# A banded retention layer with an FP4 feed-forward: corner blocks and the last 64 feed-forward columns packed into two passes, and value tiles split in eight steps

## The reference

```python
# x = X;  GAMMA = 0.9;  ln = layer norm without weights
Q, K, V = xpos(ln(x) @ W_Q), xpos(ln(x) @ W_K, downscale=True), ln(x) @ W_V
p = softmax(Q @ K.T) * 0.9 ** abs(n - m)        # decay AFTER the softmax
x = x + p @ V
g, u = fp4(ln(x)) @ fp4(w_gate).T, fp4(ln(x)) @ fp4(w_up).T   # 256 -> 704
x = x + fp4(silu(g) * u) @ fp4(w_down).T                       # 704 -> 256
# fp4: blocks of 16 columns share a scale max|x|/6, values rounded to 0,.5,1,1.5,2,3,4,6
```

## Time and profile before

| | |
|---|---|
| median of 3 runs | 2677.11 us (2676.68 to 2681.3) |
| the profiled execution | 2681.48 us, of which the span is 2679.4 us |
| PE matmul / weight load busy | 97% / 87% of the span |
| DVE / ACT / POOL busy | 81% / 57% / 67% |
| granted TensorE clock | 0.994 of full speed over the span |
| DMA | 184.11 MB, queue busy 19.9% of 16 engines |
| chain that ended last | PE 69%, POOL 8%, issue 4%, DVE 3%, ACT 2% |

### The profile page before, as it was taken

The page is one execution under the profiler, slowest core; times in us unless marked ns, Lnnn a source line. Parts: engine busy times, 40 slices in busy tenths (PEclk is TensorE's granted clock), DMA queues, the critical chain, the costliest instruction groups (busy, mean ns, idle before and its releaser), DMA issues.

```text
span 2679.4 us, 51414 instructions
## 1 busy us (share of the span) xinstructions
PE 2610.4 (97%) x16418; PEld 2343.5 (87%) x16418; DVE 2173.3 (81%) x4784; ACT 1514.3 (57%) x2936; POOL 1794.8 (67%) x1635
## 2 busy tenths in 40 slices
PE   8999999999999999999999999999999999999997
PEld 7888789988998889988998899888998899889986
DVE  8999777778888888788888888788878888888885
ACT  5666555555555555555555555555555555565553
POOL 6999846667666666666666666666666666666664
PEclk9999999999999999999999999999999999999998
DMA  7878400121001300120002100130013001210000
GB/s 275 288 274 284 177 13 23 30 91 41 25 27 32 103 25 19 33 101 29 25 31 91 40 25 27 32 103 25 19 33 102 28 25 33 91 39 25 27 24 17
DMA packets 136033, 184.11 MB, mean 69 GB/s; under 512 B 10080, under 2 KB 93152, under 8 KB 135776
## 3 DMA queue, kind: packets, MB, share of 16 engines
q1 hardware_dynamic: 135776, 180.85, 19.9%
HBM read 103.22 MB, written 77.59 MB: 67 GB/s over the span
## 4 chain that ended last, share of the span: by engine, by line
PE 69%; POOL 8%; issue 4%; DVE 3%; ACT 2%; POOLq 0%; DVEq 0%; ACTq 0%
PE score L420 21%; PE acc L539 17%; PE ring L420 15%; PE acc L420 8%; PE ring L512 5%; PE ring L557 3%; POOL vals L838 2%; POOL h_buf L877 2%; POOL probs L856 2%; POOL hq_buf L881 1%; PE ring L504 1%; POOL xv L862 1%; DVE smax L1079 1%; ACT probs L703 1%; ACT hT L673 1%
## 5 line engine op out<-in xcount | busy, mean ns | idle before, releaser
L856 POOL TENSOR_TENSOR probs<-probs,decay 128x512 f32<-128x512 f32 (+3 forms) x432 | 523.9, 1229 | 437.7 <-ACT probs L703 437.7
L420 PE MATMUL score<-keys,q_st 128*128 128x512 f32 x3072 | 770.8, 400 | 6.0 <-ACT probs L703 3.2
L420 PEld LDWEIGHTS score<-keys,q_st 128*128 128x128 f32 x3072 | 561.2, 189 | 122.5 <-issue 3.6
L539 PE MATMUL acc<-vals,pT 128*128 128x256 f32 x4416 | 588.9, 285 | 1.6 <-DVE pT L1066 1.6
L539 PEld LDWEIGHTS acc<-vals,pT 128*128 128x128 f32 x4416 | 552.7, 189 | 14.3 <-DVE pT L1066 2.9
L420 PE MATMUL ring<-w_gu,xqT 128*128 128x512 f32 (+1 forms) x2304 | 508.6, 374 | 0.0
L1079 DVE TENSOR_REDUCE smax<-score 128x1 f32<-128x1024 f32 x256 | 313.2, 1224 | 220.1 <-PE score L420 218.3
L673 ACT ACTIVATE pT<-ring 128x512 fp32r<-128x512 f32 (+3 forms) x432 | 226.7, 535 | 451.1 <-PE ring L512 443.6
L420 PEld LDWEIGHTS ring<-w_gu,xqT 128*128 128x128 f32 x2304 | 419.2, 188 | 62.1
L862 POOL TENSOR_TENSOR xv<-xv,xe 128x256 f32<-128x256 f32 x128 | 94.4, 737 | 336.1 <-DVE xv L935 336.1
L1066 DVE TENSOR_TENSOR pT<-ring,pT 128x512 fp32r<-128x512 f32 (+3 forms) x432 | 251.0, 606 | 71.8 <-ACT pT L673 71.7
(11 more groups left out here) (121 smaller groups left out, 4096.4 us busy)
## 6 DMA issues: line engine op xcount, KB each, us to landing
k_dram<-keys SPq DMA_DIRECT2D x56, 512.0 KB, 4.7
keys<-k_dram SPq DMA_DIRECT2D x56, 512.0 KB, 7.3
q_raw<-q_dram SPq DMA_DIRECT2D x129, 128.0 KB, 2.5
x_in<-X SPq DMA_DIRECT2D x32, 512.0 KB, 4.5
q_dram<-q_stage SPq DMA_DIRECT2D x32, 512.0 KB, 5.6
x_res<-X SPq DMA_DIRECT2D x128, 128.0 KB, 2.0
out<-x_res SPq DMA_DIRECT2D x128, 128.0 KB, 1.7
v_raw<-v_dram SPq DMA_DIRECT2D x29, 512.0 KB, 3.5
```

Source lines behind the costliest of these rows:

```text
L420: mm = pe.matmul(dst, stat(a, k), mov(m, k), start=i == 0, stop=i == n - 1)
L539: mm = pe.matmul(pv_out, pT[g % 2][:, a, j * P:(j + 1) * P], vals[m][:, kb, :], start=i == 0, stop=i == n - 1)
L856: pool.tensor_tensor(probs[:, k0 * P:k1 * P], probs[:, k0 * P:k1 * P], decay[:, off:off + (k1 - k0) * P], ALU.mult).then_inc(decayed, 1)
```

## The change

Three edits, in one version:

1. **Corners.** The outermost blocks of the band (`CORNERS`, 18 a batch: kb = t-7 for t >= 7, kb = t+7 for t <= 8) have 64 keys that count. Their probabilities are written twice side by side into `edge_probs` (GpSimd, one operation with the 64 columns repeated), so that the transposed block has the 64 keys twice on its 128 rows. `edge` holds the upper part of those 64 value rows above the lower part. Then two matmuls (upper and lower part of the probabilities) give all of what three gave, and lower x lower besides. `edge` is filled from `vals` by two DMAs of 64 rows for each corner (`load_edges`, on SyncE, two buffers). A group with a corner has one more operation in `decays` and one block fewer in the other.
2. **The last 64 of the 704 columns** go the same way: GpSimd writes columns 640 to 703 of `hq` twice (128 columns) and the first 640 in a second operation; the last weight block is upper over lower (one DMA in step 1 of batch 0); `down` takes 17 matmuls in place of 18. The transposes of `hq` remain 6. Two memsets ahead of the stage go.
3. **Values** are split 2 blocks at a time: `V_SPLIT = (10, 12, 14, 0, 1, 3, 5, 7)`. The order of the loads follows.

```diff
-V_SPLIT = (T - 3, 0, 1, 4)
+V_SPLIT = (10, 12, 14, 0, 1, 3, 5, 7)
+NV, VT = len(V_SPLIT), T // len(V_SPLIT)
+CORNERS = [(t, kb) for t in range(T) for kb in (t - BAND, t + BAND) if 0 <= kb < T]
+EDGES = 2
...
+            def load_edges(j, t, is_first):
+                for u, (x, kb) in enumerate(CORNERS):
+                    if x == t:
+                        if not is_first and (t == 0 or kb % VT == 0 and kb > t):
+                            sp.wait_ge(v_parted, (j - 1) * NV + kb // VT + 1)
+                        elif u >= EDGES:
+                            sp.wait_ge(pv_done, j * T + CORNERS[u - EDGES][0] + 1)
+                        r = corner_key(t, kb)
+                        for i in range(2):
+                            sp.dma_start(edge[u % EDGES][i * HALF:(i + 1) * HALF, :].bitcast(F32),
+                                         vals[i][r:r + HALF, kb, :].bitcast(F32)).then_inc(edge_loaded[u % EDGES], 16)
...
-                        for a, m in PASSES:
-                            mm = pe.matmul(pv_out, pT[g % 2][:, a, j * P:(j + 1) * P], vals[m][:, kb, :],
+                        if kb in edges:
+                            place, loads = edges[kb]
+                            pe.wait_ge(edge_loaded[place], loads * 32)
+                        for a, m in ((0, 0), (1, 0)) if kb in edges else PASSES:
+                            mm = pe.matmul(pv_out, pT[g % 2][:, a, j * P:(j + 1) * P], edge[place][:] if kb in edges else vals[m][:, kb, :],
...
-                    product(dn_out, lambda a, k: hT[a][:, k, :], lambda m, k: w_dn[m][:, k, :],
-                            range(HK)).then_inc(dn_done, 1)
+                    product(dn_out, lambda a, k: hT[a][:, k, :], lambda m, k: w_dn[m][:, k, :], range(HK - 1), False)
+                    for a in range(2):
+                        mm = pe.matmul(dn_out, hT[a][:, HK - 1, :], w_dn[0][:, HK - 1, :], start=False, stop=a == 1)
+                    mm.then_inc(dn_done, 1)
...
+                    for kb in bs:
+                        if (s, kb) in CORNERS:
+                            k0 = kb * P + corner_key(s, kb)
+                            op = pool.tensor_tensor(edge_probs[:, int(kb > s), :].rearrange("p (a k) -> p a k", a=2), twice(probs[:, k0:k0 + HALF]),
+                                               twice(decay[:, off + k0:off + k0 + HALF]), ALU.mult)
...
-                    pool.tensor_tensor(blocks(hq[t % 2]), blocks(hv[t % 2]), spread(hs[t % 2][:], HB), ALU.mult).then_inc(hq_ready, 1)
+                    pool.tensor_tensor(hq[t % 2][:, F - HALF:FT].rearrange("p (a b k) -> p a b k", a=2, k=QB), last, scale, ALU.mult)
+                    pool.tensor_tensor(blocks(hq[t % 2][:, 0:F - HALF]), blocks(hv[t % 2][:, 0:F - HALF]), spread(hs[t % 2][:, 0:HB - n], HB - n), ALU.mult).then_inc(hq_ready, 1)
```

More of the change, by code:

```diff
@@ L31 @@
 HCOL = [min(k * P, F - P) for k in range(HK)]
+HALF = P // 2
+FT = F + HALF
+assert F == (HK - 1) * P + HALF and BAND * P + P - (HALF - 1) - 1 >= ZERO_FROM
 WC = F * D // P
@@ L163, in build @@
         v_raw = [sb(f"v_raw{i}", [P, CT, D]) for i in range(2)]
-        decay = sb("decay", [P, ND * P])
+        decay = sb("decay", [P, ND * P - 2 * HALF])
+        edge, edge_probs = [sb(f"edge{i}", [P, D], F32R) for i in range(EDGES)], sb("edge_probs", [P, 2, P])
         xqT = [sb(f"xqT{i}", [P, KT, P], F32R) for i in range(2)]
@@ L193, in build @@
         q_back = [sem(f"q_back{i}") for i in range(2)]
+        edge_loaded = [sem(f"edge_loaded{i}") for i in range(EDGES)]
         res_loaded = [sem(f"res_loaded{i}") for i in range(4)]
@@ L222, in values_at @@
         def values_at(at, s):
-            return [c for c in range(NC) if s == V_SPLIT[c] and (c == 0 or at[2] is loop_plan)]
+            return [h for h in range(NV) if s == V_SPLIT[h] and (h < 3 or at[2] is loop_plan)]
         def tile(at, t):
@@ L240, in pieces_before, with edges_at @@
             return at[0] * sum(per) + (sum(per[:t]) if t >= 0 else sum(per[:t + T]) - sum(per))
+        def edges_at(at, t):
+            batch = at[0] if t >= 0 else at[0] - 1
+            return {kb: (u % EDGES, batch * (len(CORNERS) // EDGES) + u // EDGES + 1) for u, (x, kb) in enumerate(CORNERS) if x == t % T}
         def blocks(ap):
@@ L381, in step @@
                         load_keys(j, c)
-                if s == V_SPLIT[0] - 3:
+                if s == 8:
                     load_values(j + 1, 0, not is_first, more)
-                if s == T - 2 and more:
-                    load_values(j + 1, 1, not is_first)
-                if s in (0, V_SPLIT[1] + 1) and not is_first:
-                    load_values(j, 3 if s else 2)
+                if s == 11:
+                    load_values(j + 1, 1, not is_first, more)
+                if s == 13 and more:
+                    load_values(j + 1, 2)
+                if s == 1 and not is_first:
+                    load_values(j, 3)
+                load_edges(j, s, is_first)
                 if s >= XR or not is_first:
@@ L413, in _, with product @@
         def _(pe):
-            def product(dst, stat, mov, ks):
+            def product(dst, stat, mov, ks, ends=True):
                 n = len(ks) * len(PASSES)
@@ L419, in product @@
                     for a, m in PASSES:
-                        mm = pe.matmul(dst, stat(a, k), mov(m, k), start=i == 0, stop=i == n - 1)
+                        mm = pe.matmul(dst, stat(a, k), mov(m, k), start=i == 0, stop=ends and i == n - 1)
                         i += 1
@@ L525, in attend @@
                 gs = groups(t % T)
-                n, i = len(band(t % T)) * len(PASSES), 0
+                edges = edges_at(at, t)
+                n, i = len(band(t % T)) * len(PASSES) - len(edges), 0
                 batch = at[0] if t >= 0 else at[0] - 1
@@ L853, in decays @@
                         meanwhile()
-                    k0, k1 = bs[0], bs[-1] + 1
-                    off = (k0 - s + BAND) * P
-                    pool.tensor_tensor(probs[:, k0 * P:k1 * P], probs[:, k0 * P:k1 * P],
-                                       decay[:, off:off + (k1 - k0) * P], ALU.mult).then_inc(decayed, 1)
+                    off = (BAND - s) * P - HALF
+                    for kb in bs:
[3 more added lines that the diff above has]
+                                               twice(decay[:, off + k0:off + k0 + HALF]), ALU.mult)
+                    whole = [kb for kb in bs if (s, kb) not in CORNERS]
+                    if whole:
+                        k0, k1 = whole[0] * P, (whole[-1] + 1) * P
+                        op = pool.tensor_tensor(probs[:, k0:k1], probs[:, k0:k1], decay[:, off + k0:off + k1], ALU.mult)
+                    op.then_inc(decayed, 1)
             def x_quantised(at, t):
@@ L880, in h_quantised @@
                     pool.wait_ge(h_levelled, g + 1)
-                    pool.tensor_tensor(blocks(hq[t % 2]), blocks(hv[t % 2]), spread(hs[t % 2][:], HB), ALU.mult).then_inc(hq_ready, 1)
+                    n = HALF // QB
+                    last, scale = (x[:, -n:].unsqueeze(1).to_broadcast([P, 2, n, QB]) for x in (blocks(hv[t % 2]), spread(hs[t % 2][:], HB)))
+                    pool.tensor_tensor(hq[t % 2][:, F - HALF:FT].rearrange("p (a b k) -> p a b k", a=2, k=QB), last, scale, ALU.mult)
+                    pool.tensor_tensor(blocks(hq[t % 2][:, 0:F - HALF]), blocks(hv[t % 2][:, 0:F - HALF]), spread(hs[t % 2][:, 0:HB - n], HB - n), ALU.mult).then_inc(hq_ready, 1)
             def step(at, s):
@@ L889, in step @@
                     rstd_tile(at, s - 1)
-                for c in values_at(at, s):
-                    values(at, c)
+                for h in values_at(at, s):
+                    values(at, h)
                 x_quantised(at, s - 1)
```

55 lines of the change are left out of this document (31 added, 24 removed).

## The result

| | before | after |
|---|---|---|
| median of the runs of one comparison, us | 2676.89 (2672.93 to 2681.3, 4 runs) | 2649.52 (2645.47 to 2650.19, 4 runs) |
| profiled execution, us (span) | 2681.5 (2679.4) | 2649.03 (2647.2) |
| mean granted clock of the profile | 0.994 | 0.995 |
| one turn of the batch loop, us | 290.03 | 286.16 to 286.44 |

The ratio is 0.9891, 95% interval [0.9879, 0.9903]: 27.4 us less between the medians, 32.5 us less between the two profiled executions. Forecast were 2644, and 32.6 less on the profile. The total came out; two of its parts didn't, and they nearly cancel. That the two profiled executions agree with the forecast to 0.1 us is luck as well: the one of before was 4.4 us over its median, and 1.4 us of the difference lie ahead of the tile stage, whose first scores come between 345.4 and 351.8 us in the runs here other than e3 and e5.

The account below looks back on a forecast made before the run. TensorE was taken to bound the tile stage. Terms -32.4 + 2.8 - 3.5 + 0.5 (memsets, smaller decay table, last four steps) = -32.6 us, from the median 2677.1 to 2644; 8 in 10 range 2632 to 2660.

Parts of the forecast that it names:

- Matmuls, -32.4 and +2.8: TensorE: corners save 17.1 us and `down` 15.3, together 32.4; 2.8 lost where a corner matmul saved is waited away.
- the rooms: Time by which `hq` is early in steps without a split: 1.29 to 2.41 us, said to cover 0.74.
- g: Growth of GpSimd's path to `hq_ready` from the added corner and `hq` operations: 0.50 us a step.
- The lower bound of about 0.2: GpSimd path growth a step if the added operations cost only their fixed part: about 0.2 us.
- The splits, -3.5: GpSimd's half value splits shorten TensorE's waits for `hq`: 0.50 us a batch in 7 batches, 3.5 us gained.
- at nothing: Price given to halving ScalarE's copies of the values, ScalarE being 56% busy.
- the forecast 0.15: Loss in steps 4 and 13 together, same load, with room nearer that of step 3: 0.15 us.
- Step 15, -0.4 forecast: A split comes in before TensorE's step 15: `hq` 0.86 us late, 0.45 waited anyway, loss 0.4.
- Copies to `edge`: 288 DMAs of 64 KB on SyncE, wanted at least 11.5 us later: cost 0, up to 3 us in tile 15's step.
- Rival D: A copy to `edge` is late, tile 15's or small waits at every corner: 2658 to 2665 us; chance 0.08.
- 7.3 plus 2.0: Time set for tile 15's `edge` copy behind eight key loads, in us, against 11 us until its use.
- Rival B: Half splits fit GpSimd's idle time before `xv`, all split stalls go: 15 us more, 2629; chance 0.10.

Follow-up runs that it names:

- e3: Changed kernel with 64 more instructions at TensorE's start, waiting for `ident_in`, which shift the loop in its instruction blocks; ratio to before 0.9869, a turn 284.44 to 284.63 us.
- e5: Kernel before with 178 waiting instructions at TensorE's start, putting its loop's end where the changed kernel has it; 2695.18 us in one run, a turn 290.07 to 291.32.
- e10: Changed kernel without its corners (all band blocks in three passes); 2653.84 us in one run, a turn 286.14 to 286.25.
- e11: Changed kernel without the packed last 64 columns (`down` in 18 matmuls, `hq` in one operation); 2653.81 us in one run, a turn 286.36 to 286.42.
- e1: Kernel before with only the new `V_SPLIT` (values split 2 blocks at a time); ratio to before 0.9954, a turn 288.08 to 288.17 us.
- e8: Changed kernel with 64 more instructions at TensorE's start on a semaphore set early, so they cost no time; 2638.24 us, ratio to before 0.9849.
- e4: Changed kernel without reloading the keys' lower halves, so half of the 4 MB of key loads; 2643.29 us in one run, a turn 284.52 to 285.12.
- e12: Changed kernel with 8 early-passing wait instructions ahead of TensorE's loop; 2641.91 us in one run, a turn 284.54 to 285.13.
- e7: Changed kernel with one more GpSimd operation of 704 columns (1.39 us) ahead of `hq` in every step; ratio to before 1.0145, a turn 293.1 to 296.2 us.

## Why the prediction was right

- **Matmuls, -32.4 and +2.8**: right. 1.66 and 1.86 us a turn are 3.5, against 3.7 forecast (e10, e11; the earlier trace rows gave the price); the two corners of a step gave 0.21 in place of 0.24. The corner with its operation, the two of `hq` and the rooms held: no wait for `hq` stands in steps 3 to 12 of the turn shown.
- **g**: priced 0.50. In steps 1 and 2, behind half splits, the path is 9.61 and 9.88 with packing and 9.23 and 9.50 without (e1): 0.38. The added path counted in no other step. The lower bound of about 0.2 was wrong by its own prices: two fixed parts of 0.18 are 0.36, and the measured g stands just above that.
- **The splits, -3.5**: the term that was mis-sized. The whole of it was to be 0.5 us a turn. The stalls that went are 1.09 less 0.20 that then waits for `xqT`, and 1.40 less 0.46: 1.8, with 0.1 in step 14 1.9. Two things were missed. In step 1 I took VectorE's obstruction as the length of the split, from the one row, and didn't see that in the step before the 16-column scaling was caught in place of the 256-column one, with 0.64 us more behind it. ScalarE's halved copies, priced "at nothing", are what freed it by the rows above, though no run tests that by itself. And in step 2 I let TensorE come 0.24 us sooner to a path of fixed start. From step 1's first `hq` transposes on, TensorE took 16.10 us to those of step 2 before and 16.25 after: two matmuls fewer, but step 1's second bank now waits for `xqT`. The path's start kept its distance from the same transposes (the end of `rstd` 6.75 us behind them, then 6.69), so it moved forward with the stall that went. So the stall fell by 0.94 where the path fell by 0.74. Steps 4 and 13 lost nothing of the forecast 0.15.
- **Step 15, -0.4 forecast**: nothing of it. Its first bank has no wait for `hq`, only 0.42 for `xqT`, as before (0.45).
- **Copies to `edge`**: 2.0 us in the median, 9.6 at the longest, beside the keys; never waited for. Rival D falls, though its 7.3 plus 2.0 was about the longest.
- **Rival B** came nearly true in its effect, not in its cause: half splits still stand in the path (`xv` scaled in 1.07 beside them, 0.47 alone), but short enough for TensorE not to notice outside step 2. It supposed 15 us more than the forecast; about 9 were there, and were seen only once the new wait was gone (e8).
- **What no step of mine had**: six waits of 1.5 to 1.7 us for instructions, 9.5 in all. I looked at the loads in step 15 for the copies that queue behind them, and not for who else uses the same 16 engines.

So 4.2 us a turn were expected (2.14 and 1.90 of matmuls, 0.35 lost, 0.50 of splits) and 5.5 arrived, less some 1.8 for a cause outside the sum: 3.7. The total was right by luck, because an error of 9 us and one of 10.6 (six turns at 1.8) nearly cancel; the matmuls, the larger part, were right by their mechanism. That the new waits are for an instruction fetch rests on its constant distance from the scores that wait, and on the first way into the loop, which has the loads and no fetch. That the key loads hold it up is shown as far as half of the loads brings it sooner (e4) and a shift in the program removes or shrinks the waits (e3, e8, e12); when a fetch is asked for no row shows. Which block is late for a given placing can be read from a trace, but not yet forecast (e5).

## What to carry to other kernels

Price a shortening of a co-running operation by the order in which the other engine meets it, in each step by itself: 0.31 us late or 0.14 early decided 0.64. An engine that is 56% busy can set that order, as ScalarE's copy did here. Let a stall that you shorten pull the start of the path it waits for along, when that start hangs on the same engine. And after any edit that changes the number of instructions in a loop, look for waits on "issue" at its start; if bulk loads run there, moving the loop in the program by some instructions that pass while the engine idles anyway can be worth as much as a tuned operation. Where an edit makes TensorE wait longer, look at its granted clock behind the wait before all of the loss is put down to the wait.

## What was not expected of the hardware

- TensorE waited 1.47 to 1.67 us in each of six turns for an instruction fetch, while loads filled the 16 DMA engines at about 400 GB/s; half of the loads left 0.6 us in all, 64 instructions ahead of the loop removed it and 8 left 1.0 us in all.
- The 16-column scaling on VectorE took 0.23 us, and 2.12 with a 2.41 us subtraction on GpSimd beside it that had begun 0.31 us sooner; 0.14 us ahead of one it took its 0.23.
- In e7 the granted TensorE clock fell to 0.50 for 3.4 us behind eight of its waits of 2.0 to 2.2 us, 1.4 to 1.6 us lost each time; behind others as long (2.10 to 2.28) it stayed at 1.00.
- A 64 KB copy inside SBUF lands in 2.0 us, and in 8.7 behind 4 MB of loads.
- An instruction that waits for a semaphore long past took about 0.11 us: 64 of them passed in the 10.5 us that TensorE idles at its start (e8), 178 made those 20.1 us (e5), and 64 on one that is set late began the work 6 us later (e3).
